# Raw expert weights in two places, loaded two experts ahead, and their load tables made one tile per partition

## The chip, the cores and the metric

The kernel runs on one core of one Trainium2 chip. The metric is the device time of one execution in microseconds; smaller is better. Engines are named as in the profile: PE (matmuls), DVE (vector), ACT (scalar), POOL (GpSimd), SP (which issues most of the DMAs here).

## What is computed

Two gated layers over x of 16 x 128 tokens with 512 features. The first three parts (cross attention with 16 heads, a ternary linear layer, a sigmoid attention over features) are not touched. The fourth is a mixture of 16 experts on 2048 tokens, with two shared experts:

```python
scores = jax.nn.sigmoid(xf @ gate_w.T)                 # [2048, 16]
...                                                    # best 2 of 4 groups, best 4 experts of these
cw = jnp.zeros((T, E), x.dtype).at[jnp.arange(T)[:, None], idx].add(w)
h = jax.nn.silu(jnp.einsum('td,edh->teh', xf, w1)) * jnp.einsum('td,edh->teh', xf, w3)
y = jnp.einsum('teh,ehd,te->td', h, w2, cw)
z = jax.nn.silu(xf @ sw1) * (xf @ sw3) @ sw2
return (y + z).reshape(b, s, d)
```

An expert has W1 and W3 of 512 x 352 and W2 of 352 x 512, all float32. The kernel computes y for the chosen four experts of a token only.

## The kernel before

**Order of the program.** Three blocks run one after the other: `attention_heads_and_ternary`, `attention_features`, `experts`. The last has two stages, `routing_and_shared_expert` and `expert_tiles`. Inside a stage every engine has its own list of instructions, written out by hand; semaphores are the only order between engines, and an engine that waits holds up all that stands behind on its list.

**Tiles.** Tokens are sorted by expert into tiles of 128 rows, each expert's share filled up to whole tiles; with these inputs 68 tiles are in use, in 17 trips of four (`UT`). Twelve experts get tiles. With tiles numbered from 0, an expert's first tile is one of 0, 1, 2, 7, 23, 28, 31, 35, 36, 44, 53, 62, so that three experts have one tile only (tiles 0, 1 and 35).

**A tile n in `expert_tiles`.** All products are made in three passes from a high and a low part of each operand. PE multiplies the rows by W1 and W3 (24 matmuls, `t_H`, L1738), transposes the rows of tile n+1 (`t_TX`, L1717), multiplies tile n-1 by W2 (`t_Y`, L62 to L64) and transposes the hidden rows of tile n (`t_TH`, L1750). ACT makes SiLU (L1783) and the high part of each operand, DVE the product (L1837) and the low parts; x of the next tile is L1760 on ACT and L1812 on DVE.

**The expert weights.** SP loads raw W1 and W3 into `r13` (L990) and raw W2 into `r2` (L995, L996); both are called `m_r` in the profile, and there is one place for each. ACT and DVE split them into `W13` and `W2` (`m_W`): W13 of tile n+1's expert during tile n (L1764 on ACT, L1816 on DVE), W2 of tile n's expert at the end of tile n (L1797, L1798; L1850, L1853). When tile n is the first of its expert, SP waits until W13 of that expert is split (`w13_lo`), so that `r13` is free, and issues W1 and W3 of the next expert; then it waits for the W2 split and issues W2. So a load starts at the first tile of the expert before.

**What a tile needs to know.** `m_meta` in SBUF holds for each tile whether it is the first of its expert, and the next expert; each engine reads these numbers into registers (a TENSOR_LOAD and a few register operations) and branches on them. DVE and ACT read one number at each tile (L1834, L1780), and two more at the start of a trip (L1829 and L1831 on DVE). They stand ahead of the tile's first instruction, the copy `t_wcol` (L1835) on DVE and the SiLU on ACT.

**Where `m_meta` is made.** In `routing_and_shared_expert` the shared expert runs as 24 chunks q: `hidden(q)` on PE, `gated(q)` on ACT and DVE, and after three of them `outer(u)` on PE. `hidden(q)` waits for `gated(q-2)`'s first step, because the banks A and B are double. DVE does the routing between chunks, by the table `between`; q = 10, 11 and 12 make the numbers of all 83 columns in every partition, as operations of 128 x 1328 elements. From q = 12 on DVE also makes rows for a one-hot product on PE (`table`, L1493 and L1495; PE's `tables`, L1268), which yields the row numbers of every tile.

Of the kernel before, what the change touches and what calls it, by code (L numbers as in the profile page):

```python
# [15 lines left out]
P = 128  # L16
# [20 lines left out]
IC = [P, P, I - 2 * P]  # L37

# [923 lines left out]
def experts(nc, c, gate_w, ebias, w1, w2, w3, sw1, sw2, sw3, out):  # L962
# [7 lines left out]
    with ExitStack() as st:  # L970
        def sb(name, shape, dt=F32):
            return st.enter_context(nc.sbuf_tensor(name, shape, dt))
        m = dict(meta=sb("m_meta", [1, 3, NT + 3], I32),
# [13 lines left out]
def load_expert(sp, m, w1, w3, e, done):  # L987

    for j, w in enumerate((w1, w3)):
        sp.dma_start(m["r13"][:, :, j, :], w[bass.ds(e, 1)].rearrange("e (k p) i -> p (e k) i", p=P)).then_inc(done, 16)  # L990


def load_expert_out(sp, m, w2, e, done):

    sp.dma_start(m["r2"][:, 0:2, :], w2[bass.ds(e, 1), 0:2 * P, :].rearrange("e (k p) i -> p (e k) i", p=P)).then_inc(done, 16)  # L995
    sp.dma_start(m["r2"][0:IC[2], 2, :], w2[bass.ds(e, 1), 2 * P:I, :].rearrange("e p i -> p (e i)")).then_inc(done, 16)  # L996

# [11 lines left out]
def routing_and_shared_expert(nc, c, m, gate_w, ebias, w1, w2, w3, sw1, sw2, sw3):  # L1009
# [4 lines left out]
    with ExitStack() as st:  # L1014
# [8 lines left out]
        XT = sb("XT", [P, 2, KC, NB * S], F32R)  # L1023
        r1, r3, r2 = m["r13"][:, :, 0, :], m["r13"][:, :, 1, :], m["r2"][:, :, :]
# [14 lines left out]
        J = NT + 3  # L1039
        iE = sb("r_iE", [P, E])  # L1040
        iJ = sb("r_iJ", [P, NT + 3])
# [21 lines left out]
        for W_, n, k, w in ((W1, "W1", KC, I), (W3, "W3", KC, I), (W2, "W2", 3, D)):  # L1063
# [11 lines left out]
        ti = early[:, NB * 20:NB * 20 + NT + 3].bitcast(I32)  # L1075
# [3 lines left out]
        first, nxt = big[:, NB * TOPK * E:NB * TOPK * E + J], big[:, NB * TOPK * E + J:]  # L1079
# [4 lines left out]
                                    "meta_ok", "pads_in"))  # L1084
        row_out = [sem(f"e_row_out{b}") for b in range(NX)]
# [22 lines left out]
        with nc.Block() as block:  # L1108
            @block.sync
            def _(sp):  # L1110
# [23 lines left out]
                sp.wait_ge(x2_in, 32)  # L1134
                for g in range(NG):
# [54 lines left out]
            def _(pe):  # L1190
# [6 lines left out]
                def logit(g):  # L1197
# [7 lines left out]
                    for k in range(KC):  # L1205
                        i = mm3(pe, L[0:E, :], lambda h_: gwT[:, h_, k, :],
                                lambda h_: XT[:, h_, k, g * GT:(g + 1) * GT], k == 0, k == KC - 1)
# [9 lines left out]
                def hidden(q):  # L1217
# [8 lines left out]
                    for W_, bk in ((W1[b], A[q % 2]), (W3[b], B[q % 2])):  # L1226
                        for k in range(KC):
                            x_ = mm3(pe, bk[0:IC[ch], :], lambda j: W_[:, j, k, cols],
                                     lambda j: XT[:, j, k, gr * GT:(gr + 1) * GT], k == 0, k == KC - 1)
# [42 lines left out]

                def counts():
# [31 lines left out]
            def _(act):  # L1305
# [20 lines left out]
                for t in range(NB):  # L1326
                    act.wait_ge(t_fill, t + 1)
                    act.activation(XT[:, 0, :, t * P:(t + 1) * P], T[t % 2][:, :].rearrange("p (k n) -> p k n", k=KC),
# [10 lines left out]
                for q in range(3, 3 * NU):  # L1339
# [8 lines left out]
                    if q == SPLIT_AT[2]:  # L1348
                        act.wait_ge(meta_ok, 1)
                    if q in SPLIT_AT:  # L1350
                        split_hi(1, SPLIT_AT.index(q))
                    if q in EXPERT_AT:
# [3 lines left out]
                        act.activation(m["W13"][:, 0, k, :, :], m["r13"][:, k, :, :], ACT.Copy).then_inc(x13_hi, 1)  # L1356

            @block.vector
            def _(dve):
                done = 1  # L1360

                def step(instr):
                    nonlocal done
                    done += 1
                    instr.then_inc(routed, 1)
# [9 lines left out]
                je = [P, J, E]  # L1375
                cmp = eq[:, :].rearrange("p (j e) -> p j e", j=J)
                ej = big[:, 0:J]
# [128 lines left out]
                def tile_experts():  # L1506

                    step(dve.tensor_tensor(cmp, upto.unsqueeze(1).to_broadcast(je), iJ[:, :].unsqueeze(2).to_broadcast(je),
                                           ALU.is_le))
                    step(dve.tensor_reduce(ej, cmp, AX.X, ALU.add))  # L1510
                    step(dve.tensor_scalar(ej, ej, float(E - 1), None, ALU.min))
                    step(dve.memset(first[:, 0:1], 1.0))
                    step(dve.tensor_tensor(first[:, 1:J], ej[:, 1:J], ej[:, 0:J - 1], ALU.not_equal))

                def next_candidates():

                    step(dve.tensor_scalar(far, nt, 0.5, 1000.0, ALU.is_lt, ALU.mult))
                    step(dve.tensor_tensor(far, far, iE[:, :], ALU.add))
                    step(dve.tensor_tensor(cmp, iE[:, :].unsqueeze(1).to_broadcast(je), ej.unsqueeze(2).to_broadcast(je),
                                           ALU.is_le))  # L1520
                    step(dve.tensor_scalar(cmp, cmp, 1000.0, None, ALU.mult))

                def next_expert():
                    step(dve.tensor_tensor(cmp, cmp, far.unsqueeze(1).to_broadcast(je), ALU.add))
                    step(dve.tensor_reduce(nxt, cmp, AX.X, ALU.min))
# [362 lines left out]
```

## Time and profile before

| | |
|---|---|
| median of 3 runs | 1371.61 us (1370.1 to 1372.55) |
| the profiled execution | 1371.29 us, of it 1369.6 us from first to last instruction |
| mean granted PE clock | 0.954 of 2.4 GHz |
| PE busy | 1230.6 us (90%) |
| DVE, ACT, POOL busy | 719.2, 553.2, 424.0 us |
| stage of routing and shared expert | about 584 to 844 us of the span |
| tiles of the experts | 846 to 1347 us |

PE is the engine that is busy nearly throughout, so what counts is where it stands still and where its clock is at the lower level. The profile gives for each instruction the idle time of its engine before it and who ended it.

### The profile page before, as it was taken

The page shows a single profiled execution, that of the slowest core. Times are in us where ns is not written, and L with a number is a line of the kernel's source. Part 1 is how long each engine was busy: PE and PEld are TensorE (multiplying, and loading weights), DVE is VectorE, ACT ScalarE, POOL GpSimd, SP SyncE. Part 2 cuts the span into 40 slices and gives each one's busy share as a digit, 9 for nine tenths or more (in the row PEclk, how much of TensorE's full clock was granted, in tenths as well). Part 3 has the DMA queues.
Part 4 walks back from the last instruction along what each step waited for, and adds up shares of the span by engine and source line. Part 5 has one row for each costly group of instructions (what it writes and reads, how often), then busy time and mean ns, then how long its engine had stood idle before and what let it go on. Part 6 is the DMA issues. An engine that isn't in the chain of part 4 may idle for free. (4 is left out here: it accounts for less than half of the span.)

```text
span 1369.6 us, 25480 instructions
## 1 busy us (share of the span) xinstructions
PE 1230.6 (90%) x7821; PEld 1034.4 (76%) x7822; DVE 719.2 (53%) x1443; ACT 553.2 (40%) x1430; POOL 424.0 (31%) x504
## 2 busy tenths in 40 slices
PE   6998999999997399969998998699999989999992
PEld 6876777777776177746776876699999878999992
DVE  5666655656645589953677643442334443424340
ACT  4543444444444188833121111543344443434341
POOL 1101211211211556540005721235444433444442
PEclk9999999999998699979999999899999999999997
DMA  9000000000000111143000204555446755545456
GB/s 326 25 16 19 17 1 18 17 1 17 1 2 1 33 45 38 38 141 118 0 1 0 94 31 137 159 129 100 77 80 141 195 142 116 132 86 135 86 140 169
DMA packets 53880, 103.62 MB, mean 76 GB/s; under 512 B 5126, under 2 KB 20998, under 8 KB 53750
## 3 DMA queue, kind: packets, MB, share of 16 engines
q1 hardware_dynamic: 38182, 65.78, 14.7%
q0 software_dynamic: 15632, 36.97, 14.3%
q8 instruction: 40, 0.66, 0.2%
q14 instruction: 26, 0.21, 0.1%
HBM read 75.99 MB, written 30.93 MB: 78 GB/s over the span
## 5 line engine op out<-in xcount | busy, mean ns | idle before, releaser
L1738 PE MATMUL t_H<-m_W,t_xT 128*128 128x352 f32 x1632 | 286.4, 332 | 16.7 <-DVE m_W L1816 13.9
L1738 PEld LDWEIGHTS t_H<-m_W,t_xT 128*128 128x128 f32 x1632 | 268.0, 193 | 18.7 <-DVE m_W L1816 14.8
L1705 POOL DMA_INDIRECT acc_d<-t_ys,t_sid x68 | 109.2, 1606 | 279.0 <-ACT t_ys L1767 191.5
L1783 ACT ACTIVATE t_sl<-t_H 128x352 f32<-128x352 f32 x68 | 31.5, 463 | 175.4 <-PE t_H L1738 173.7
L597 ACT ACTIVATE pr<-pr 128x128 f32<-128x128 f32 x256 | 76.0, 298 | 55.2 <-DVE pr L758 53.9
L62 PE MATMUL t_Y<-m_W,t_hT 128*128 128x512 f32 (+1 forms) x207 | 88.2, 426 | 9.4 <-DVE t_hT L1861 6.4
L1837 DVE TENSOR_TENSOR t_h<-t_H,t_sl 128x352 f32<-128x352 f32 x68 | 35.5, 523 | 106.5 <-ACT t_sl L1783 106.5
L1767 ACT ACTIVATE t_ys<-t_Y,t_wcol 128x512 f32<-128x512 f32 x69 | 47.3, 685 | 94.8 <-PE t_Y L64 94.8
L1859 DVE TENSOR_TENSOR t_hT<-t_TH,t_hT 128x256 fp32r<-128x256 f32 x68 | 28.7, 422 | 107.1 <-ACT t_hT L1804 105.9
L64 PE MATMUL t_Y<-m_W,t_hT 128*128 128x512 f32 (+1 forms) x207 | 82.3, 397 | 0.0
L63 PE MATMUL t_Y<-m_W,t_hT 128*128 128x512 f32 (+1 forms) x207 | 82.0, 396 | 0.0
L386 POOL TENSOR_TENSOR X<-X,upd 128x512 f32<-128x512 f32 x16 | 20.3, 1269 | 160.0 <-DVE upd L737 160.0
L373 POOL TENSOR_TENSOR tmp<-tmp,nhalf 128x2 f32<-128x2 f32 (+2 forms) x22 | 18.6, 846 | 143.0 <-DVE tmp L627 119.2
L1174 POOL TENSOR_SCALAR m_W<-m_W,bst 128x128 fp32r<-128x128 f32 x64 | 52.0, 830 | 34.5 <-PE eL L1268 34.4
L753 DVE TENSOR_REDUCE mx<-SC 128x4 f32<-128x512 f32 x64 | 43.7, 683 | 32.7 <-PE SC L517 32.6
L569 ACT ACTIVATE pT<-T 128x512 f32<-128x512 f32 x64 | 38.0, 594 | 53.9 <-PE T L423 53.6
L1323 ACT ACTIVATE ehT<-eh 128x512 fp32r<-128x512 f32 (+1 forms) x24 | 15.2, 632 | 93.9 <-DVE eh L1543 93.9
L62 PEld LDWEIGHTS t_Y<-m_W,t_hT 128*128 128x128 f32 (+1 forms) x207 | 39.2, 189 | 16.6 <-DVE m_W L1853 7.0
L1812 DVE TENSOR_TENSOR t_xT<-t_TX,t_xT 128x512 fp32r<-128x512 f32 x69 | 47.6, 690 | 4.8 <-ACT t_xT L1760 2.3
L597 ACT ACTIVATION_READ_ACCUMULATOR pr<-pr 128x1 f32 x256 | 47.8, 187 | 0.0
L845 DVE TENSOR_TENSOR as<-asg,as 128x512 fp32r<-128x512 f32 x66 | 44.2, 688 | 4.4 <-ACT as L901 4.4
L64 PEld LDWEIGHTS t_Y<-m_W,t_hT 128*128 128x128 f32 (+1 forms) x207 | 39.0, 188 | 9.7
(415 smaller groups left out, 3229.6 us busy)
## 6 DMA issues: line engine op xcount, KB each, us to landing
m_r<-in_L_ffn_w_dram SPq DMA_DIRECT2D x26, 704.0 KB, 5.1
m_r<-in_L_ffn_w_dram SPq DMA_DIRECT2D x13, 512.0 KB, 3.9
aCX<-in_ctx_dram SPq DMA_DIRECT2D x20, 256.0 KB, 2.6
rows_d<-before_w SPq DMA_DIRECT2D x17, 256.0 KB, 2.0
CT<-in_ctx_dram SPq DMA_DIRECT2D x8, 512.0 KB, 3.8
X<-in_x_dram SPq DMA_DIRECT2D x4, 1024.0 KB, 13.0
acc_d<-X SPq DMA_DIRECT2D x4, 1024.0 KB, 4.2
m_r<-in_L_ffn_sw_dram SPq DMA_DIRECT2D x4, 704.0 KB, 5.4
```

Of the source, the lines that this page charges most:

```text
L62: pe.matmul(out, lhs(0), rhs(0), start=first, stop=False)
L63: pe.matmul(out, lhs(0), rhs(1), start=False, stop=False)
L64: return pe.matmul(out, lhs(1), rhs(0), start=False, stop=last)
L569: act.activation(pT[:, t % 2, :, :].rearrange("p j m -> p (j m)"), src, ACT.Copy).then_inc(t_hi, 1)
L597: i = act.activation(pp, pp, ACT.Exp, scale=SCALE0, accum_out=sums[:, t // HQ % 2, at_:at_ + 1])
L753: dve.tensor_reduce(mx[:, t % 2, :], bk, AX.X, ALU.max).then_inc(s_out, 1)
L845: dve.tensor_tensor(s[:, m % KC, 1, :], sg[:, m % KC, :], s[:, m % KC, 0, :].bitcast(F32), ALU.subtract)\
L1174: i = pool.tensor_scalar(tab_a[t % SLOTS][:, k, :], iP.bitcast(F32), place_p[:, t, k:k + 1], None, ALU.is_equal)
L1705: pool.indirect_dma_start(out=m["acc_d"][:, :], out_offset=bass.IndirectOffsetOnAxis(ap=sid[:, b:b + 1], axis=0), in_=ys[:, b, :], in_offs ...
L1738: x_ = pe.matmul(bk[b % 2][:, 0:I], xT[:, b % 2, jx, k, :], W13[:, jw, k, j, :], start=k == 0 and jx == jw, stop=k == KC - 1 and jx == 1)
L1767: act.activation(ys[:, (b - 1) % UT, :], Y[(b - 1) % 2][:, :], ACT.Copy, scale=wcol[:, (b - 1) % UT:(b - 1) % UT + 1]).then_inc(y_evac, 1)
L1812: dve.tensor_tensor(xT[:, b % 2, 1, :, :], TX[:, :].rearrange("p (k t) -> p k t", k=KC), xT[:, b % 2, 0, :, :].bitcast(F32), ALU.subtract) ...
```

## The change

**Places.** `m_raw` holds two experts' raw W1, W3 and W2 side by side. The second place lies where the stage before keeps its transposed rows `XT`; so `XT` is laid out group by group, and the second expert is loaded when the two groups under it have been used for the last time. Before the tiles start, the experts of the first two groups of tiles are loaded; at the first tile of an expert SP issues the load of the expert after the next, into the place of the present one. SP now also waits for the load before to have landed.

**Numbers.** ACT, DVE and SP read which place: two more register loads at each tile on ACT and DVE, one more on SP. The addresses of the splits and loads come from a register.

**Tables.** In place of operations over 83 x 16 columns in every partition, each partition works out the numbers of one tile, in operations of 16 columns or 1, up to four at once without a wait (`tile_columns`, at q = 10). PE turns the four resulting columns into rows (`tile_rows`, after `hidden(11)`), and DVE writes them to `m_meta` (at q = 11). Nothing of this is left at q = 12.

```diff
-                 r13=sb("m_r13", [P, KC, 2, I]), r2=sb("m_r2", [P, 3, D]),
+        with ExitStack() as shortly:
+            m["raw"] = shortly.enter_context(nc.sbuf_tensor("m_raw", [P, 2, RAW], F32))
+        sb("m_raw_first", [P, RAW])
...
-        XT = sb("XT", [P, 2, KC, NB * S], F32R)
+        XT = sb("XT", [P, NG, 2, KC, GT], F32R)
...
@@ SP, routing stage @@
-                sp.wait_ge(meta_ok, 1)
-                e0 = sp.value_load(m["meta"][0:1, 2, 0:1], min_val=0, max_val=E - 1)
-                load_expert(sp, m, w1, w3, e0, x13_in)
-                load_expert_out(sp, m, w2, e0, x2_in)
-                sp.wait_ge(x2_in, 32)
+                sp.wait_ge(meta_ok, 2)
+                one, two = (sp.value_load(m["meta"][0:1, at:at + 1], min_val=0, max_val=E - 1) for at in (AT_ONE, AT_TWO))
+                load_expert(sp, m, w1, w3, one, slice(0, 1), x13_in)
+                load_expert_out(sp, m, w2, one, slice(0, 1), x2_in)
+                sp.wait_ge(ab_fill, 3 * (NG + 2))
+                sp.wait_ge(x13_in, 32)
+                load_expert(sp, m, w1, w3, two, slice(1, 2), x13_in)
+                sp.wait_ge(x2_in, 32)
+                load_expert_out(sp, m, w2, two, slice(1, 2), x2_in)
...
@@ PE, routing stage @@
+                def tile_rows():
+                    pe.wait_ge(meta_ok, 1)
+                    for n in range(4):
+                        i = pe.matmul(CP[0:1, n * P:(n + 1) * P], cols[:, n:n + 1], c["identF"][:, :], start=True, stop=True)
+                    i.then_inc(meta_ps, 1)
...
                             hidden(q)
                             if q == 7:
                                 counts()
+                            if q == 11:
+                                tile_rows()
...
@@ DVE, routing stage @@
+                def tile_columns():
+                    step(dve.tensor_scalar(filled, nt, 0.5, None, ALU.is_gt),
+                         dve.tensor_tensor(begin, upto, nt, ALU.subtract),
+                         dve.tensor_scalar(passed, upto, mine, None, ALU.is_le),
+                         dve.tensor_scalar(use, mine, float(UT), upto[:, E - 1:E], ALU.mult, ALU.is_lt))
...
-                           8: expert_starts, 9: table_rows, 10: tile_experts, 11: next_candidates, 12: next_expert}
+                           8: expert_starts, 9: table_rows, 10: tile_columns, 11: tile_rows}
...
@@ SP, tiles @@
+                            place = bass.ds(sp.value_load(m["meta"][0:1, bass.ds(n + AT_PLACE, 1)], min_val=0, max_val=1), 1)
                             with sp.If(first):
+                                sp.wait_ge(r13_in, 32 * (n + 2))
+                                sp.sem_inc(own_sp, 1)
                                 sp.wait_ge(w13_lo, 4 * (n + 1))
                                 sp.sem_inc(own_sp, 1)
-                                load_expert(sp, m, w1, w3, nxt, r13_in)
+                                load_expert(sp, m, w1, w3, nxt, place, r13_in)
+                                sp.wait_ge(r2_in, 32 * (n + 2))
+                                sp.sem_inc(own_sp, 1)
                                 sp.wait_ge(w2_lo, 2 * (n + 1) + 2)
                                 sp.sem_inc(own_sp, 1)
-                                load_expert_out(sp, m, w2, nxt, r2_in)
+                                load_expert_out(sp, m, w2, nxt, place, r2_in)
...
@@ DVE, tiles (ACT alike) @@
-                            this, first = first, dve.value_load(m["meta"][0:1, 0, bass.ds(n + 1, 1)], min_val=0, max_val=1)
+                            this, first = first, dve.value_load(m["meta"][0:1, bass.ds(n + 1, 1)], min_val=0, max_val=1)
+                            here, there = (bass.ds(dve.value_load(m["meta"][0:1, bass.ds(n + AT_PLACE + a, 1)], min_val=0, max_val=1), 1)
+                                           for a in range(2))
                             dve.tensor_copy(wcol[:, b:b + 1], wgt[:, bass.ds(n, 1)])
...
-                    dve.tensor_tensor(W13[:, 1, k, :, :], r13[:, k, :, :], W13[:, 0, k, :, :].bitcast(F32), ALU.subtract)\
+                    dve.tensor_tensor(W13[:, 1, k, :, :], raw13(m, place)[:, k, :, :], W13[:, 0, k, :, :].bitcast(F32), ALU.subtract)\
```

Of the changed kernel's PE list, this is the end of `hidden(11)` (banks `eB`) and the start of `hidden(12)` (`eA` with the second shared expert's weights `eW`); line numbers are those of the changed kernel, and `before_w` holds the four columns.

```order
L66 MATMUL eB<-XT,m_W 96x512
L67 MATMUL eB<-XT,m_W 96x512
L68 MATMUL eB<-XT,m_W 96x512
L1299 MATMUL eC<-identF,before_w 1x128 [waits e_meta_ok]
L1299 MATMUL eC<-identF,before_w 1x128 x3
L66 MATMUL eA<-XT,eW 128x512 [waits eb_out,ew_lo]
L67 MATMUL eA<-XT,eW 128x512
```

Before, `hidden(12)` stands directly behind `hidden(11)`; now four small matmuls that wait for DVE's `tile_columns` stand between.

On DVE the same place is q = 10 to q = 11. Before, between the steps of `gated(10)` (L1545) and `gated(11)` (L1543):

```order
L1545 TENSOR_TENSOR ehT<-eh,ehT 128x512 [waits eh_hi]
L1508 TENSOR_TENSOR before_w<-r_n,r_iJ 128x1328
L1510 TENSOR_REDUCE before_w<-before_w 128x83 [waits e_routed]
L1511 TENSOR_SCALAR before_w<-before_w 128x83 [waits e_routed]
L1512 MEMSET before_w 128x1 [waits e_routed]
L1513 TENSOR_TENSOR before_w<-before_w 128x82 [waits e_routed]
L1543 TENSOR_TENSOR eh<-eB,m_first 96x512 [waits eh_lo,ea_out,e_routed]
```

In the changed kernel 20 operations stand there, in eight groups; these are the first groups and the last three groups:

```order
L1542 TENSOR_SCALAR before_w<-r_n 128x16
L1543 TENSOR_TENSOR before_w<-r_n 128x16
L1544 TENSOR_SCALAR before_w<-r_n,r_tok 128x16
L1545 TENSOR_SCALAR before_w<-r_tok,r_n 128x1
L1546 TENSOR_SCALAR r_n<-before_w 128x16 [waits e_routed]
...
L1558 TENSOR_SCALAR before_w<-r_iE,before_w 128x16 [waits e_routed]
L1559 SCALAR_TENSOR_TENSOR before_w<-before_w 128x1
L1560 TENSOR_TENSOR before_w<-before_w,r_n 128x16 [waits e_routed]
L1561 TENSOR_REDUCE before_w<-before_w 128x1 [waits e_routed]
L1583 TENSOR_TENSOR eh<-eB,m_first 96x512 [waits eh_lo,ea_out]
```

Five operations, two of them wide, have become twenty narrow ones, and the last of them is what PE waits for.

On DVE in the tiles, between the low parts of tile n's hidden rows (L1909 and L1911) and the product of tile n+1 (L1887), the changed kernel has:

```order
L1911 TENSOR_TENSOR t_hT<-t_TH,t_hT 96x128
L1882 ISA
L1882 TENSOR_LOAD m_meta
L1882 ISA x2
L1883 TENSOR_LOAD m_meta
L1883 ISA x3
L1883 TENSOR_LOAD m_meta
L1883 ISA x2
L1885 REGISTER_ALU
L1885 COPY t_wcol<-m_wgt 128x1
L1887 TENSOR_TENSOR t_h<-t_H,t_sl 128x352 [waits t_silu]
```

Before, only the first of the three register loads (TENSOR_LOAD) stood there.

## Rows read from the trace of the kernel before

**Rows 1.** PE by time, tiles 9 and 13: start us, us, engine, line, operation.

```profile
927.36 4.10 PE L1738 MATMUL t_H<-m_W,t_xT 128*128 128x352 f32 x24
...
954.31 4.08 PE L1738 MATMUL t_H<-m_W,t_xT 128*128 128x352 f32 x24
```

**Rows 2.** The same view, tile 1 to tile 4; in brackets the idle before.

```profile
859.23 4.14 PE L1738 MATMUL t_H<-m_W,t_xT 128*128 128x352 f32 x24
...
864.45 0.48 PE L62 MATMUL t_Y<-m_W,t_hT 128*128 128x512 f32 x1 [0.64 <-DVE t_hT L1861]
...
874.88 6.11 PE L1738 MATMUL t_H<-m_W,t_xT 128*128 128x352 f32 x24 [7.76 <-DVE m_W L1816]
...
890.64 0.47 PE L62 MATMUL t_Y<-m_W,t_hT 128*128 128x512 f32 x1 [2.47 <-DVE t_hT L1861]
...
893.07 4.10 PE L1738 MATMUL t_H<-m_W,t_xT 128*128 128x352 f32 x24
```

**Rows 3.** The same view, tile 35 to tile 38.

```profile
1104.70 4.14 PE L1738 MATMUL t_H<-m_W,t_xT 128*128 128x352 f32 x24
...
1117.82 5.84 PE L1738 MATMUL t_H<-m_W,t_xT 128*128 128x352 f32 x24 [6.10 <-DVE m_W L1816]
...
1134.16 0.47 PE L62 MATMUL t_Y<-m_W,t_hT 128*128 128x512 f32 x1 [3.31 <-DVE t_hT L1861]
...
1137.67 4.57 PE L1738 MATMUL t_H<-m_W,t_xT 128*128 128x352 f32 x24
```

**Rows 4.** SP by time: two of the issues of raw W1 and W3.

```profile
866.68 0.93 SPq L990 DMA_DIRECT2D m_r<-in_L_ffn_w_dram  x2
...
1107.30 0.95 SPq L990 DMA_DIRECT2D m_r<-in_L_ffn_w_dram  x2
```

**Rows 5.** DVE by time, round the trip ends after tiles 7 and 11.

```profile
925.49 0.15 DVE L1835 COPY t_wcol<-m_wgt 128x1 f32 x1 [1.37 <-issue]
...
925.99 0.68 DVE L1812 TENSOR_TENSOR t_xT<-t_TX,t_xT 128x512 fp32r<-128x512 f32 x1
...
951.71 0.15 DVE L1835 COPY t_wcol<-m_wgt 128x1 f32 x1 [2.21 <-issue]
...
958.92 0.53 DVE L1837 TENSOR_TENSOR t_h<-t_H,t_sl 128x352 f32<-128x352 f32 x1 [2.31 <-ACT t_sl L1783]
```

**Rows 6.** Register loads on DVE, 948 to 955 us: duration ns, first and last start.

```profile
L1829 DVEq TENSOR_LOAD <-m_meta x1: 305/305/305, 949.4 to 949.4; - x1
...
L1834 DVEq TENSOR_LOAD <-m_meta x1: 374/374/374, 950.9 to 950.9; - x1
```

**Rows 7.** PE by time, in the stage of routing and shared expert.

```profile
717.86 0.40 PE L64 MATMUL eB<-XT,m_W 128*96 128x512 f32 x1
...
725.34 0.47 PE L62 MATMUL eY<-m_W,ehT 128*128 128x512 f32 x1 [1.42 <-issue]
...
742.72 1.15 PE L1268 MATMUL eL<-m_W 128*128 128x240 f32 x4 [3.30 <-DVE m_W L1495]
744.32 1.18 PE L1268 MATMUL eL<-m_W 128*128 128x240 f32 x4 [0.45 <-DVE m_W L1495]
```

**Rows 8.** DVE by time, where it makes the tables for the loads.

```profile
719.29 1.63 DVE L1508 TENSOR_TENSOR before_w<-r_n,r_iJ 128x1328 f32<-128x1328 f32 x1
...
723.17 0.69 DVE L1543 TENSOR_TENSOR eh<-eB,m_first 96x512 f32<-96x512 f32 x1
...
736.57 1.53 DVE L1524 TENSOR_TENSOR before_w<-before_w,r_n 128x1328 f32<-128x1328 f32 x1
```

**Rows 9.** DVE by time: three small operations without a wait between, then the next.

```profile
583.74 0.19 DVE L109 TENSOR_TENSOR mean<-bst 128x16 f32<-128x16 f32 x1 [0.30 <-PEq L812]
...
584.15 0.17 DVE L112 TENSOR_SCALAR mean<-mean 128x16 f32<-128x16 f32 x1
```

**Rows 10.** By stretch: its us, busy us of PE, PEld, DVE, ACT, POOL; clock, DMA, GB/s.

```profile
742.80:749.70 6.90, 6.46 (x19) 4.71 (x20) 6.10 (x9) 1.58 (x2) 5.73 (x6) 0.51 0.01 2
...
1135.00:1139.00 4.00, 4.00 (x15) 3.35 (x14) 0.20 (x1) 1.23 (x3) 0.06 (x1) 0.57 0.50 172
```

More of the change, by code:

```diff
@@ L37 @@
 IC = [P, P, I - 2 * P]
+RAW = 2 * KC * I + 3 * D
+AT_FIRST, AT_NEXT, AT_PLACE, AT_USE = 0, NT + 1, 2 * NT + 1, 3 * NT + 2
+AT_ONE, AT_TWO, AT_TRIPS = AT_USE + TRIPS, AT_USE + TRIPS + 1, AT_USE + TRIPS + 2
+META = AT_TRIPS + 1
 class Count:
@@ L1355, in _ @@
                         act.wait_ge(tab_used, NB)
-                        act.activation(m["W13"][:, 0, k, :, :], m["r13"][:, k, :, :], ACT.Copy).then_inc(x13_hi, 1)
+                        act.activation(m["W13"][:, 0, k, :, :], r13[:, k, :, :], ACT.Copy).then_inc(x13_hi, 1)
             @block.vector
@@ L1360, in _, with step @@
                 done = 1
-                def step(instr):
+                def step(*instrs):
                     nonlocal done
-                    done += 1
-                    instr.then_inc(routed, 1)
+                    for instr in instrs:
+                        instr.then_inc(routed, 1)
+                    done += len(instrs)
                     dve.wait_ge(routed, done)
@@ L1374, in _ @@
                 pl = run[:, 1, :, :]
-                je = [P, J, E]
-                cmp = eq[:, :].rearrange("p (j e) -> p j e", j=J)
-                ej = big[:, 0:J]
+                filled, begin, passed, both, cand, col = (spare_cols[:, n * E:(n + 1) * E] for n in range(6))
+                here, nxt, half = (col[:, n:n + 1] for n in (4, 5, 6))
                 def best_groups():
@@ new lines, in tile_rows @@
+                def tile_rows():
+                    dve.wait_ge(meta_ps, 1)
+                    for n, (at, w) in enumerate(((AT_FIRST, NT + 1), (AT_NEXT, NT), (AT_PLACE, NT + 1), (AT_USE, TRIPS))):
+                        dve.tensor_scalar(m["meta"][:, at:at + w], CP[0:1, n * P:n * P + w], float(E - 1), None, ALU.min)
+                    dve.tensor_scalar(m["meta"][:, AT_ONE:AT_ONE + 1], here[0:1, :], float(E - 1), None, ALU.min)
+                    dve.tensor_scalar(m["meta"][:, AT_TWO:AT_TWO + 1], nxt[0:1, :], float(E - 1), None, ALU.min)
+                    step(dve.tensor_scalar(half[0:1, :], upto[0:1, E - 1:E], 1.0 / UT, 0.5 - 0.5 / UT, ALU.mult, ALU.add))
+                    dve.tensor_scalar(m["meta"][:, AT_TRIPS:AT_TRIPS + 1], half[0:1, :], ROUND, -ROUND, ALU.add, ALU.add)\
+                        .then_inc(meta_ok, 1)
@@ L1616, in bank @@
             return [st.enter_context(nc.psum_tensor(f"{name}{i}", [P, 512], F32)) for i in range(n)]
-        rowid, wgt, r13, r2, W13, W2 = (m[n] for n in ("rowid", "wgt", "r13", "r2", "W13", "W2"))
+        rowid, wgt, W13, W2 = (m[n] for n in ("rowid", "wgt", "W13", "W2"))
+        sb("t_raw_second", [P, RAW])
         sid = sb("t_sid", [P, UT], U32)
@@ L1760, in x_hi, with w13 @@
                     act.activation(xT[:, b % 2, 0, :, :], TX[:, :].rearrange("p (k t) -> p k t", k=KC), ACT.Copy).then_inc(tx_hi, 1)
-                def w13():
+                def w13(place):
                     for k in range(KC):
-                        act.activation(W13[:, 0, k, :, :], r13[:, k, :, :], ACT.Copy).then_inc(w13_hi, 1)
+                        act.activation(W13[:, 0, k, :, :], raw13(m, place)[:, k, :, :], ACT.Copy).then_inc(w13_hi, 1)
                 def y_out(b):
@@ L1787, in _ @@
                                 act.wait_ge(r13_in, 32 * (n + 2))
-                                w13()
+                                w13(there)
                             with act.Else():
@@ L1842, in _ @@
                                     dve.wait_ge(w13_hi, 4 * (n + 1) + k + 1)
-                                    w13_k(k)
+                                    w13_k(k, there)
                             with dve.Else():
```

139 lines of the change are left out of this document (73 added, 66 removed).

## The prediction

> **What bounds the kernel.** I read the page first: PE is busy 90% of the span, so I looked for the places where PE stands still or runs at the lower clock. Then I read PE in order of time through the tiles. In the steady state four tiles take 954.31 - 927.36 = 26.95 us, 6.74 each, without a gap [rows 1]. Twice it is otherwise. From the start of tile 1 to that of tile 4 it takes 893.07 - 859.23 = 33.84 us instead of 20.2 [rows 2]: PE waits 7.76 us for split W13 ahead of tile 2, 2.47 us for a hidden row that stands behind the W2 split on ACT and DVE, and the 24 matmuls of tile 2 take 6.11 us instead of 4.14, as the clock has fallen. From tile 35 to tile 38 it takes 1137.67 - 1104.70 = 32.97 us [rows 3], with waits of 6.10 and 3.31 us and again one slow group. Both follow an expert of one tile. The issues on SP say why: the weights that tile 2 lacks were asked for at 866.68, when tile 1 was already running, and those of tile 36 at 1107.30, inside tile 35 [rows 4]. Elsewhere an expert has at least two tiles, and its successor's load is back in time.
>
> The third place is in the routing stage. PE stops for 3.30 and 0.45 us ahead of the one-hot products [rows 7], since DVE makes the load tables first (from 736.57, [rows 8]); behind it the clock is at half for 6.9 us [rows 10].
>
> **The change, part by part.**
>
> *Late loads.* With two places the load that started at 866.68 starts one expert earlier, and so do the others; tiles 2 and 36 find their weights split as soon as ACT and DVE come to them. What is late next is the splitting itself: tiles 0, 1 and 35 each split W2 for themselves and W13 for the next one. Tile 0 does this today with everything landed, and PE waits 0.64 us for it [rows 2]. I keep that, and give tile 1, which starts with DVE behind, 0.9. Front: 33.84 - 20.2 - 0.64 - 0.9 = 12.1 us, rounded to 12.0. Tile 35 gets 0.9 too, and it is also the last of a trip, where the register loads (below) come on top of the split: 1.6. Middle: 32.97 - 20.2 - 0.9 - 1.6 = 10.3 us. The start of tile 0 stays as it is. Bounds: no wait left gives 13.6 + 12.8 = 26.4, and 2 us more in each place gives 18.
>
> *Register loads.* DVE now reads three numbers ahead of a tile instead of one, and five instead of three at a trip's start. Three loads start 950.9 - 949.4 = 1.5 us apart from first to last, so one costs 0.75 us [rows 6], and two more 1.5. In a tile inside a trip DVE idles 2.31 us for SiLU behind them [rows 5], so they are hidden, and what they cost without that cover is 1.5 us a tile. At a trip's start they already take all the time: the copy stands 2.21 us behind the last work for "issue", at 951.71. From the copy to the end of the next x on DVE it takes 925.99 + 0.68 - 925.49 = 1.18 us [rows 5]. With 1.5 us more this x would be ready at 954.39, and PE wants it at 954.31 [rows 1]: 0.1 us a trip. Where a split stands in the tile before the trip's start, DVE comes later. After tile 7 x was ready at 926.67 and PE began at 927.36; with 1.5 more it begins at 928.17, 0.8 us late. Such trip ends are those after tiles 7, 23 and 31 (W2) and 27 and 43 (W13); the one after 35 is in the middle's sum. So 5 x 0.8 + 10 x 0.1 = 5.0 us lost. Bounds: nothing (if the loads run ahead) and twice that.
>
> The Trainium skill, page "DMA: Bandwidth & Descriptors", section "Latency and other measured facts", gives a floor of some 600 ns for a tensor_load. Here the load itself is shorter (305 to 374 ns [rows 6]), and with its register operations it takes 0.75 us; by the page's figure two cost 1.2, the loss would be about 3 us, and the estimate of the time about 1351.
>
> *Tables.* At q = 12 the work from 736.57 goes away, and the rows for PE are made at once. PE's wait of 3.30 + 0.45 us and the half clock behind it go: of 6.9 us PE is busy 6.46 [rows 10], which at the full clock is 3.2 us less. Gain 6.95 us. But `tile_rows` puts a wait on PE in front of `hidden(12)`. PE comes to it at 718.26 [rows 7]; DVE only starts `tile_columns` at 719.29, where the old table code starts today [rows 8]. Three operations of 128 x 16 issued together take 584.15 - 583.74 = 0.41 us [rows 9], about 0.21 for a group and 0.1 for each further one; 20 in eight groups take 8 x 0.21 + 12 x 0.1 = 2.9 us. So PE stands still until 722.2, 4 us, makes four small products (0.45 us; four of 240 columns took 1.15 at the low clock [rows 7], and these have 128) and begins `hidden(12)` 4.5 us later than today. Queued behind it is `outer(3)`, which today waits 1.42 us for DVE before 725.34 [rows 7]; that wait is swallowed, so it starts 3.1 us late. A stand of 4 us is longer than the 3.30 and 3.31 us after which the clock fell [rows 3, 7, 10], so I expect it to fall here too. The price is half the time at the low clock: 1.7 us after tile 37 (4.0 us at 0.57) and 3.2 at 742.8; I take 2.1, nearer to the first, since here no second wait follows. Together 5.2 lost, 6.95 won: 1.75 us gained. Bounds: if the clock holds 3.85; if each of the 20 operations takes 0.21 us and the clock costs 3.2, a loss of 0.7.
>
> *Free.* The second load before the tiles lies under the shared expert's last chunks on PE, and SP's stores behind it are wanted only when all is stored. The layout of `XT` keeps the same 512 columns in a row for PE. SP's extra register load and waits stand where SP has been idle.
>
> *Sum.* 12.0 + 10.3 - 5.0 + 1.7 = 19.0 us. The profiled execution took 1371.29, which gives 1352.3; it lies 0.3 below the median, so 1352.6.
>
> **The rivals.**
>
> *All cover holds.* The register loads run ahead on DVE and ACT while they wait, and the clock holds through the stand at 718: 26.4 less some 2 of splitting, plus 3.85, gives 28 us, 1343.5. For it speaks that inside a trip they are covered; against it the 2.21 us of "issue" at the trip's start.
>
> *The loads stay late.* SP takes its list in order, and a load of W1 and W3 now stands behind waits for the load before and for the W2 split. If tile 36's weights still came after tile 35 began, only the tables and the register loads would change: 1370 to 1375. Against it: the W2 split that SP waits for ends in the same tile, and two experts ahead of tile 36 are four tiles, some 27 us.
>
> *The register loads decide, and it is slower.* They stand ahead of the first instruction of every tile, on ACT and DVE. Inside a trip the cover is the 2.31 us of idle on DVE, and some 0.9 more: x is ready about 958.92 + 1.2 = 960.1, and PE wants it at 954.31 + 6.74 = 961.05 [rows 1, 5]. So two loads may cost 3.2 us, 1.6 each. Above that each tenth costs 0.2 us a tile; with some 60 tiles the 24 us of the other terms are eaten up at 1.8 us a load, and at 2.0 the time is near 1395. The place is the copy at L1835. For it: at a trip's start the copy waits 2.21 us for nothing else. Against it: 0.75 us a load in the steady state.
>
> *Gathers get in the way.* The loads of three experts now run close together at the start, beside the gathers of rows on the same DMA engines; a gather that lands two tiles late would cost PE up to 3 us there, 1356. I count this within the main case.
>
> **How the numbers follow.** Main case 0.72, from 1347 to 1361 (the sum with the register loads from 0 to 10, the tables from -0.7 to 3.9, the gathers). All cover holds 0.15, from 1342 to 1347. Loads stay late 0.07. Register loads on the path of every tile 0.06. The range of 1344 to 1361 takes the main case and part of the second: about 0.8. From no change 0.2% can be told here, 2.7 us: faster below 1368.9, slower above 1374.4. Faster: 0.72 + 0.15 and 0.01 of the late loads, 0.88; same 0.05, from the late loads; slower 0.06 + 0.01.
>
> **What would show it.** In the profile after: no wait for `m_W` longer than 1.5 us ahead of `t_H` between tiles 0 and 4 and 35 and 38; both stretches at 21.7 to 23 us; raw weights never named as releaser of ACT. At trip starts the copy on DVE some 3.7 us behind the last work instead of 2.21, and a gap on PE ahead of `t_H` after tiles 7, 23, 27, 31 and 43. In the routing stage a PE wait of about 4 us at the four products into `eC`, a lower clock behind it, and none ahead of the one-hot products. I am wrong if PE still waits for a load, if the gaps stand at every tile, or if the wait at `eC` is 6 us or more.

## The result, and the profile after

The changed kernel takes 1357.9 us (1356.34 to 1361.29), the kernel before, timed beside it, 1372.08 (1370.1 to 1373.06): a ratio of 0.9904, 95% interval 0.9889 to 0.9919, or 14.2 us less. Timed a second time in another set it came to 1360.91 against 1371.61, ratio 0.9922 (0.9895 to 0.9948). The profiled execution took 1358.05 us with a span of 1356.2, which is 13.4 less than before.

PE by time, in the kernel after. The line numbers are those of the new file: `t_H` is L1784, `t_TX` L1763, the four table products L1299.

```profile
718.17 0.40 PE L68 MATMUL eB<-XT,m_W 128*96 128x512 f32 x1
722.67 1.87 PE L1299 MATMUL eC<-identF,before_w 128*1 128x128 f32 x8 [4.11 <-DVE before_w L1561]
724.47 0.80 PE L66 MATMUL eA<-XT,eW 128*128 128x512 f32 x1
...
844.52 0.63 PE L1763 MATMUL t_TX<-identF,m_first 128*128 128x128 f32 x4 [1.62 <-PEq L1125]
...
856.72 4.12 PE L1784 MATMUL t_H<-m_W,t_xT 128*128 128x352 f32 x24
...
861.96 0.47 PE L66 MATMUL t_Y<-m_W,t_hT 128*128 128x512 f32 x1 [0.68 <-DVE t_hT L1911]
...
864.71 4.12 PE L1784 MATMUL t_H<-m_W,t_xT 128*128 128x352 f32 x24
...
869.58 0.47 PE L66 MATMUL t_Y<-m_W,t_hT 128*128 128x512 f32 x1 [0.32 <-DVE t_hT L1911]
...
879.11 4.14 PE L1784 MATMUL t_H<-m_W,t_xT 128*128 128x352 f32 x24
...
884.35 0.66 PE L1763 MATMUL t_TX<-identF,m_first 128*128 128x128 f32 x4 [1.09 <-DMA m_first<-rows_d,m_pos]
...
943.07 4.10 PE L1784 MATMUL t_H<-m_W,t_xT 128*128 128x352 f32 x24
...
970.48 4.11 PE L1784 MATMUL t_H<-m_W,t_xT 128*128 128x352 f32 x24
...
1096.96 4.12 PE L1784 MATMUL t_H<-m_W,t_xT 128*128 128x352 f32 x24
...
1109.15 0.47 PE L66 MATMUL t_Y<-m_W,t_hT 128*128 128x512 f32 x1 [0.49 <-DVE t_hT L1911]
...
1112.47 0.55 PE L1796 MATMUL t_TH<-identF,t_h 128*128 128x128 f32 x3 [0.98 <-DVE t_h L1887]
...
1119.89 4.09 PE L1784 MATMUL t_H<-m_W,t_xT 128*128 128x352 f32 x24
...
1225.03 4.12 PE L1784 MATMUL t_H<-m_W,t_xT 128*128 128x352 f32 x24 [0.85 <-DVE m_W L1864]
```

Read it in four steps. From tile 1 to tile 4 it is 879.11 - 856.72 = 22.39 us where [rows 2] had 33.84: the wait of 7.76 for split W13 is gone, the clock stays, and two short waits for hidden rows remain. From tile 35 to 38 it is 22.93 against 32.97 [rows 3]. In the routing stage PE stands for 4.11 us ahead of the products into `eC`, and nothing is left of the waits of 3.30 and 0.45 [rows 7]. And where nothing is split, a trip from tile 13 to 17 takes 970.48 - 943.07 = 27.41 us instead of 26.95 [rows 1].

SP's issues of raw W1 and W3 after. Each is now for the expert after the next: the weights of tile 2's expert are asked for at 850.41, inside tile 0, where before they were at 866.68 [rows 4]; the issue at 865.51 is already for the expert of tile 7.

```profile
850.41 1.00 SPq L1004 DMA_DIRECT2D m_raw<-in_L_ffn_w_dram  x2
...
865.51 0.98 SPq L1004 DMA_DIRECT2D m_raw<-in_L_ffn_w_dram  x2
```

DVE by time after: the first and the last operation that makes the columns, then the start of the trip at tile 12.

```profile
719.59 0.26 DVE L1542 TENSOR_SCALAR before_w<-r_n 128x16 f32<-128x16 f32 x1
...
722.45 0.17 DVE L1561 TENSOR_REDUCE before_w<-before_w 128x1 f32<-128x16 f32 x1
...
937.54 0.28 DVE L1911 TENSOR_TENSOR t_hT<-t_TH,t_hT 96x128 fp32r<-96x128 f32 x1
941.76 0.15 DVE L1885 COPY t_wcol<-m_wgt 128x1 f32 x1 [3.94 <-issue]
...
942.26 0.68 DVE L1860 TENSOR_TENSOR t_xT<-t_TX,t_xT 128x512 fp32r<-128x512 f32 x1
```

The columns take 722.62 - 719.59 = 3.03 us. The copy stands 3.94 us behind the last work (2.21 in [rows 5]), and x of tile 13 is ready at 942.94, 0.13 before PE takes it. The stretch behind PE's stand, by stretch as in [rows 10], shows the clock, first in the kernel before, then after:

```profile
722.30:725.80 3.50, 2.08 (x10) 1.42 (x9) 2.57 (x9) 1.11 (x2) 3.50 (x7) 1.00 0.00 0
...
722.30:725.80 3.50, 3.13 (x11) 1.98 (x12) 2.48 (x12) 0.63 (x1) 3.50 (x7) 0.51 0.00 0
```

The loads of a place on DVE (duration in ns, first and last start), once at the start of the trip, once inside it:

```profile
L1883 DVEq TENSOR_LOAD <-m_meta x1: 741/741/741, 939.9 to 939.9; - x1
...
L1883 DVEq TENSOR_LOAD <-m_meta x2: 300/302/303, 944.8 to 945.5; - x2
```

Inside the trip two loads start 0.7 us apart, as in [rows 6]; at its start one of them takes 0.74. At the start of the trip at tile 64 none is slow; this is PE, the loads and DVE there:

```profile
1301.39 4.13 PE L1784 MATMUL t_H<-m_W,t_xT 128*128 128x352 f32 x24
...
L1883 DVEq TENSOR_LOAD <-m_meta x2: 300/301/302, 1305.4 to 1306.1; - x2
...
1306.84 0.15 DVE L1885 COPY t_wcol<-m_wgt 128x1 f32 x1 [3.50 <-issue]
...
1307.34 0.68 DVE L1860 TENSOR_TENSOR t_xT<-t_TX,t_xT 128x512 fp32r<-128x512 f32 x1
```

The last view is what PE waited for ahead of `t_TX` (us in total, times, longest), as far as it was the landing of a gather: 2.5 us in the tiles, before 1.6.

```profile
PE t_TX L1763 <- DMA m_first<-rows_d,m_pos: 2.0, 4, 1.1
...
PE t_TX L1763 <- DMA t_later<-rows_d,m_pos: 0.5, 1, 0.5
```

### The profile page after: what moved, and what is told of

It reads as the page before. It is cut to its first block and busy times, and to the rows that moved or that the text cites. A ratio compares the mean times of both kernels' runs of the same rounds, so it can differ in the third digit from the quotient of the medians.

```text
span 1356.2 us, 26974 instructions
## 1 busy us (share of the span) xinstructions
PE 1230.3 (91%) x7829; PEld 1027.0 (76%) x7830; DVE 710.0 (52%) x1454; ACT 552.5 (41%) x1430; POOL 420.1 (31%) x504
## 5 line engine op out<-in xcount | busy, mean ns | idle before, releaser
L1784 PE MATMUL t_H<-m_W,t_xT 128*128 128x352 f32 x1632 | 281.5, 328 | 5.5 <-issue 3.0
L1784 PEld LDWEIGHTS t_H<-m_W,t_xT 128*128 128x128 f32 x1632 | 262.6, 189 | 12.1 <-issue 4.3
L1885 DVE COPY t_wcol<-m_wgt 128x1 f32 x68 | 10.5, 154 | 134.3 <-issue 134.3
L1909 DVE TENSOR_TENSOR t_hT<-t_TH,t_hT 128x256 fp32r<-128x256 f32 x68 | 28.7, 423 | 93.2 <-ACT t_hT L1852 92.0
L1197 POOL TENSOR_SCALAR m_W<-m_W,bst 128x128 fp32r<-128x128 f32 x64 | 49.1, 786 | 35.8 <-PE eL L1291 35.7
L1887 DVE TENSOR_TENSOR t_h<-t_H,t_sl 128x352 f32<-128x352 f32 x68 | 35.4, 521 | 45.9 <-ACT t_sl L1831 45.9
L1641 DVE SCALAR_TENSOR_TENSOR X<-eY,tg,X 128x512 f32<-128x512 f32 x32 | 23.8, 751 | 49.1 <-PE eY L68 49.0
L66 PEld LDWEIGHTS t_Y<-m_W,t_hT 128*128 128x128 f32 (+1 forms) x207 | 39.0, 188 | 11.7 <-issue 3.8
```

Of the source, the lines that this page charges most:

```text
L66: pe.matmul(out, lhs(0), rhs(0), start=first, stop=False)
L1197: i = pool.tensor_scalar(tab_a[t % SLOTS][:, k, :], iP.bitcast(F32), place_p[:, t, k:k + 1], None, ALU.is_equal)
L1784: x_ = pe.matmul(bk[b % 2][:, 0:I], xT[:, b % 2, jx, k, :], W13[:, jw, k, j, :], start=k == 0 and jx == jw, stop=k == KC - 1 and jx == 1)
L1887: dve.tensor_tensor(h[:, :], H3[b % 2][:, 0:I], sl[:, :], ALU.mult).then_inc(hmul, 1)
```

## The experiments

Times vary by some us from run to run, partly ahead of everything that the change touches: PE starts the routing stage at 582 to 587 us of the span. So beside the times the table gives stretches of the profiled executions, from the start of a tile's `t_H` to that of another (us). "Rest" is tiles 4 to 35 plus 38 to 67.

| kernel | median, ratio to before (95%) | 1 to 4 | 35 to 38 | rest |
|---|---|---|---|---|
| before | 1372.08 | 33.84 | 32.97 | 408.96 |
| changed | 1357.9, 0.9904 (0.9889 to 0.9919) | 22.39 | 22.93 | 419.60 |
| loads one expert ahead | 1382.17, 1.0063 (1.0043 to 1.0083) | 35.95 | 31.15 | 418.08 |
| before, two more register loads | 1378.75, 1.0050 (1.0031 to 1.0069) | 34.53 | 31.49 | 416.14 |
| place loaded in the branch | 1355.1, 0.9871 (0.9848 to 0.9895) | 22.27 | 22.21 | 416.98 |
| products one chunk later | 1349.41, 0.9839 (0.9814 to 0.9863) | 22.31 | 23.06 | 418.60 |
| gather early | 1355.28, 0.9878 (0.9848 to 0.9908) | 22.27 | 23.20 | 416.52 |
| place packed | 1353.69, 0.9857 (0.9826 to 0.9888) | 21.75 | 21.52 | 413.87 |
| gather and scatter swapped | 1390.8, 1.0131 (1.0104 to 1.0159) | 22.16 | 22.74 | 441.52 |
| packed, products later | 1344.44, 0.9816 (0.9784 to 0.9847) | 21.52 | 21.52 | 415.99 |
| packed, products later, gather early | 1336.25, 0.9752 (0.9718 to 0.9787) | 21.77 | 21.51 | 407.73 |

**The early loads undone.**

```diff
-dve.tensor_reduce(after, cand, AX.X, ALU.min).then_inc(meta_ok, 1)
+dve.tensor_copy(after, nxt).then_inc(meta_ok, 1)
...
-load_expert(sp, m, w1, w3, two, slice(1, 2), x13_in)
...
-place = bass.ds(sp.value_load(...), 1)
+place = bass.ds(sp.value_load(...) * -1 + 1, 1)
```

(and the counts that SP waits for, one load lower)

> The changed kernel with both places, the new tables and all register loads, but each expert's raw weights asked for one expert ahead, as in the kernel before. If the early loads are what made tiles 1 to 4 and 35 to 38 shorter, the waits for split W13 ahead of tiles 2 and 36 come back with some 7.8 and 6.1 us, both stretches are back near 34 and 33 us, and the time is some 21.5 us above the changed kernel: about 1379, slower than the kernel before. If having two places is enough in itself (a load need not wait for the split of the one before), the stretches stay at 22 to 23 us and the time at about 1358.

PE by time at tiles 1, 2, 4 and 36 of this kernel:

```profile
859.07 5.67 PE L1779 MATMUL t_H<-m_W,t_xT 128*128 128x352 f32 x24 [2.09 <-DVE m_W L1859]
...
876.34 5.61 PE L1779 MATMUL t_H<-m_W,t_xT 128*128 128x352 f32 x24 [8.71 <-DVE m_W L1859]
...
895.02 4.85 PE L1779 MATMUL t_H<-m_W,t_xT 128*128 128x352 f32 x24
...
1125.86 5.46 PE L1779 MATMUL t_H<-m_W,t_xT 128*128 128x352 f32 x24 [6.50 <-DVE m_W L1859]
```

Both waits are back, a third of 2.09 us stands ahead of tile 1, and the kernel is slower than before. Two places alone win nothing; what wins is that the load starts an expert earlier. The row also prices the rest of the change: without the early loads it loses.

**Register loads alone, on the kernel before.**

```diff
 this, first = first, dve.value_load(...)
+for a in range(2):
+    dve.value_load(m["meta"][0:1, 0, bass.ds(n + a, 1)], min_val=0, max_val=1)
```

(the same on ACT)

> The kernel before with two more register loads ahead of each tile on ACT and on DVE, whose values nothing uses. If the register loads are the whole loss at the trips' ends, this costs 0.45 us at a trip without a split and 0.5 to 1.3 at one with a split, together 6 to 10 us: 1378 to 1382. If the loss comes from the two places or from their transfers, it costs at most 2 us. If the loads stand on the path of every tile it costs 30 us or more.

PE by time, tiles 13 and 17:

```profile
957.76 4.11 PE L1738 MATMUL t_H<-m_W,t_xT 128*128 128x352 f32 x24
...
985.06 4.14 PE L1738 MATMUL t_H<-m_W,t_xT 128*128 128x352 f32 x24
```

A trip without a split takes 27.30 us, 0.35 more than [rows 1]; outside the two stretches the loads cost 416.14 - 408.96 = 7.2 us. That is most of the 10.6 us which the changed kernel loses there, with no second place and no earlier transfer in sight.

**The loads put where they are used.**

```diff
-here, there = (bass.ds(dve.value_load(...n + AT_PLACE + a...), 1) for a in range(2))
 ...
 with dve.If(first):
+    there = bass.ds(dve.value_load(...n + AT_PLACE + 1...), 1)
 ...
 with dve.If(this):
+    here = bass.ds(dve.value_load(...n + AT_PLACE...), 1)
```

(the same on ACT)

> The changed kernel with the two loads of a place's number on ACT and DVE moved from the head of every tile into the branches that use them, so that a tile that splits nothing makes none. If the loads at a trip's start are what costs 0.46 us at each trip without a split and about 0.5 to 1.3 at the others, the normal trip is back to 26.95 us and the time falls by 6 to 9 us, to 1349 to 1352; the loads inside the branches stand behind work of 0.6 to 0.7 us that is already running and cost at most 0.1 a split. If the trips are longer because ACT and DVE read from a place that a register names, or because loads of two experts share the DMA engines with the gathers, nothing changes: 1358. If a load inside a branch delays the split by its full 0.7 us on ACT and on DVE, about half is given back at some 30 splits: 1356 or more.

The trip from tile 13 to 17 is back to 26.93 us, but a tile that splits W13 for the next one took 7.33 to 7.37 us (tiles 6, 22, 43, 61) instead of 6.93 to 6.98: of the expected 6 to 9 us only 2.6 are left in the rest. The loads in the branch delay the split, so the third case held beside the first.

**The place packed into the first-tile number.**

```diff
+dve.scalar_tensor_tensor(out=new, in0=place, scalar=1.0, in1=new, op0=ALU.add, op1=ALU.mult)
 ...
-here, there = (...)
 with dve.If(first):
+    there = bass.ds(first // 2, 1)
```

(and so for `here`, on ACT and on SP)

> The changed kernel with the place packed into the number that says whether a tile is its expert's first (0, 1 or 2), so that ACT and DVE make as many register loads as in the kernel before and divide in registers, inside the branches. If the loads are the loss at the trips' ends, the normal trip is back to 26.95 us as with the loads in the branches, and the 0.4 us that each split lost there is not paid: the time falls by 6 to 9 us, to 1349 to 1352. If reading the raw weights through a place named in a register costs the time, or the division costs as much as a load, it stays at 1355 as with the loads in the branches, or at 1358.

The rest falls by 419.60 - 413.87 = 5.7 us, and the split tiles cost 7.01 to 7.05. That is the register loads' part with nothing put in their place. It did not go all the way back to 408.96. The split tiles are still 0.2 us above those of the kernel before (6.81 to 6.86), and PE's waits for gathered rows ahead of `t_TX` grew from 2.5 to 3.9 us:

```profile
PE t_TX L1764 <- DMA t_later<-rows_d,m_pos: 2.0, 2, 1.8
PE t_TX L1764 <- DMA m_first<-rows_d,m_pos: 1.9, 5, 0.7
```

PE, less delayed by its x, now meets the gathers earlier.

**The products into `eC` one chunk later.**

```diff
-if q == 11:
+if q == 12:
     tile_rows()
```

(in PE's list only)

> The changed kernel with the four small products of the tables behind the next hidden chunk on PE instead of ahead of it. If the stand of 4.11 us and the half clock behind it were the price that the tables paid, PE starts that chunk at 718.3 instead of 724.5, the products come at about 723.9 with their columns ready since 722.6, and the time falls by 5 to 6 us, to about 1352.5. If DVE, not PE, sets the end of this stage (its hidden rows follow the columns), PE only waits further on, ahead of the output products: a gain of 1 to 3 us, 1355 to 1357.

PE by time: the products, `outer(3)` right behind them, and the first transpose of the tiles.

```profile
720.14 1.03 PE L1299 MATMUL eC<-identF,before_w 128*1 128x128 f32 x8
...
721.10 0.50 PE L66 MATMUL eY<-m_W,ehT 128*128 128x512 f32 x1
...
835.03 0.63 PE L1763 MATMUL t_TX<-identF,m_first 128*128 128x128 f32 x4 [1.62 <-PEq L1125]
```

There is no wait. From `outer(3)` to `t_TX` it takes 113.93 us, in the changed kernel 844.52 - 730.74 = 113.78; so the whole gain lies ahead of it. From the start of the chunk before (708.8 here, 712.9 there) to `t_TX` it is 126.2 against 131.6 us: 5.4 us, as the theory of PE's stand said. The median is 8.5 us lower; the profiled execution was 4 us ahead already at the start of that chunk, which is the spread named above.

**The gather ahead of the scatter's waits.**

```diff
 pool.wait_ge(zeroed, n * 2 + UT)
+gather(pool, m, b)
 ...
 pool.indirect_dma_start(out=m["acc_d"][:, :], ...)     # scatter
-gather(pool, m, b)
```

> The changed kernel with the gather of the rows of a tile issued on GpSimd as soon as their place is free, ahead of the scatter of the finished tile instead of behind it. In the changed kernel the last register load at six trip starts takes 0.74 us on DVE and 0.94 on ACT instead of 0.30, and ends 0.42 us behind the end of a gather's issue that runs beside it. If the gather's issue holds the load up, moving it away brings these loads back to 0.30 us, the normal trip from 27.41 to about 27.0 us, and with the waits of PE for gathered rows (some 7.6 us in all, not all on the path) the time falls by 4 to 8 us: 1350 to 1354. If the loads are slow because five engines read the same table at a trip's start, they stay at 0.74 and 0.94 and only the gather waits can go: 1354 to 1357. If the issue of the gather now stands in front of the scatter and the scatters become late, up to 3 us slower.

The waits for gathered rows ahead of `t_TX` are gone, and the rest falls by 3.1 us. (The 7.6 us of the expectation count each such wait on PE and once more on PE's weight loads; PE itself waited 2.5.) The routing stage, which this edit does not touch, took longer here: the lower clock behind PE's stand lasted on, in the view by stretch:

```profile
723.70:730.20 6.50, 6.50 (x20) 4.55 (x21) 2.13 (x10) 0.63 (x1) 4.69 (x8) 0.52 0.00 0
```

But the slow register loads stayed. POOL by time and the load, in the changed kernel:

```profile
937.32 1.61 POOL L1751 DMA_INDIRECT acc_d<-t_ys,t_sid  x1 [3.53 <-ACT t_ys L1813]
939.23 1.00 POOL L1015 DMA_INDIRECT t_later<-rows_d,m_pos  x1 [0.31 <-issue]
```

and with the early gather:

```profile
939.00 1.60 POOL L1752 DMA_INDIRECT acc_d<-t_ys,t_sid  x1 [3.00 <-ACT t_ys L1813]
...
941.71 1.00 POOL L1015 DMA_INDIRECT t_later<-rows_d,m_pos  x1 [0.79 <-POOL m_pos L1744]
```

```profile
L1883 DVEq TENSOR_LOAD <-m_meta x1: 725/725/725, 941.6 to 941.6; - x1
```

The gather's issue went from before the slow load to after its start, the load stayed slow. What did not move against it is the scatter: its issue ends at 938.93 and 940.60, the slow load starts 1.0 us later in both. My theory that the gather's issue holds the loads up fell. The other case, five engines that read one table at a trip's start, fits the time as well; the next run is for the scatter.

**Gather and scatter swapped.**

```diff
 pool.wait_ge(y_evac, n + 4)
+gather(pool, m, b)
 pool.indirect_dma_start(out=m["acc_d"][:, :], ...)     # scatter
-gather(pool, m, b)
```

> The changed kernel with the gather and the scatter of GpSimd swapped behind the same wait, so that the scatter is issued 1.0 us later. With the gather issued early, the slow register loads at the trip starts did not go: in both kernels they start within 0.5 us of the first packet of a scatter, which moves from about 939.5 to 940.5 here, while the slow loads start at 939.7 to 939.9. If the start of the scatter's transfers holds the loads up, these loads take 0.30 us, the normal trip falls from 27.41 to about 27.0 us and the time by 3 to 4 us against the changed kernel in the same call or the trace. If the loads are slow for their place in the program (the third of a tile's head at a trip's start, beside PE's transposes), they stay at 0.74 and 0.94 us and the normal trip at 27.4.

POOL by time at the start of the trip at tile 12, and register loads on DVE there:

```profile
944.44 1.00 POOL L1015 DMA_INDIRECT m_first<-rows_d,m_pos  x1 [3.41 <-DMA acc_d<-t_ys,t_sid]
945.75 1.60 POOL L1752 DMA_INDIRECT acc_d<-t_ys,t_sid  x1 [0.30 <-issue]
```

```profile
L1877 DVEq TENSOR_LOAD <-m_meta x1: 780/780/780, 948.3 to 948.3; - x1
...
L1883 DVEq TENSOR_LOAD <-m_meta x2: 300/301/302, 951.0 to 951.7; - x2
```

The loads that had been slow take 0.30 us, and another is slow, 0.9 us behind the new end of the scatter's issue. So the cause moved with the scatter, as the first theory said. The gain did not come: another load of the same trip's start is slow instead, and loads at the heads of ordinary tiles are hit too, which also speaks against five engines at a trip's start.

The kernel lost 33 us for a reason that I had not seen. By its list POOL waits for the landing of a scatter before the next pair (3.41 us here; in the changed kernel it waited for ACT instead). With that wait POOL needs 6.64 us from one gather to the next (937.80 to 944.44), nearly the 6.7 us that a tile takes PE, so that hardly any slack is left. At tiles 8, 45 and 63, where raw weights are being loaded, the wait is 6.97 to 7.21 us:

```profile
916.61 1.00 POOL L1015 DMA_INDIRECT m_first<-rows_d,m_pos  x1 [7.10 <-DMA acc_d<-t_ys,t_sid]
```

PE then waits 5.28 us for this gather and 16.4 us in all for rows; these three tiles lose 19 of the 22 us that the rest lost, and 6 us more stand behind the last tile. In this profile 5 us of the 33 stand ahead of the tiles, which the swap does not touch.

**All that helped, together.** Packed number and later products; then the early gather too.

> Two of the three edits of the fastest kernel so far: the place packed into the first-tile number and the four products behind the next hidden chunk, with the gather left behind the scatter. If the early gather is worth the waits for rows on PE, this is 3 to 5 us slower than with all three, 1339 to 1342. If the packed number leaves little for the gather, 1336 to 1338.

> Three edits on the changed kernel together: the place packed into the first-tile number, the four products of the tables behind the next hidden chunk, and the gather issued ahead of the scatter. If each takes away a loss of its own, the gains add up: 6 to 9, 6 to 8 and 2 to 5 us, so 1336 to 1344. If the packed number already takes the loads away from the gather, the gather's part is only that of the waits for rows: 1341 to 1346. If one of the three returns the others' gains, it is no faster than the products alone, 1349.

With three edits the kernel takes 1336.25 us, 35.4 less than before and 24.7 less than the changed kernel timed beside it.

The gains add up, and more: the gather is worth 3.1 us on the changed kernel and 415.99 - 407.73 = 8.3 on the packed one, whose PE comes earlier for its rows. The rest is now 1.2 us shorter than before the change, and the kernel before waited for gathers as well. I had put it at 1336 to 1344, and the run without the early gather at 1339 to 1342; that one came to 1344.44.

**The changed kernel again.**

> The changed kernel as it is, timed beside the others on the same chip: 1358, or 14 us below the kernel before, as the first time. If the chip of this call gives another distance, the edits are to be compared with this run and not with the first one.

It lay 10.7 us below the kernel before, in an interval that overlaps the first.

## Why the prediction was right, and where not

It said 1352.6, in a range of 1344 to 1361, and faster with 0.88; it is faster, at 1357.9. In spans the sum promised 19.0 us and 13.4 came.

- **Late loads, front and middle: right.** 12.0 and 10.3 forecast, 33.84 - 22.39 = 11.45 and 32.97 - 22.93 = 10.04 measured. PE waits for `m_W` in neither stretch, and ACT never for raw weights (15.0 us in three places before). The run with the loads one expert ahead shows that it is the earlier load and not the second place. What is late next is the splitting, as said: 0.68, 0.32, 0.49 and 0.98 us.
- **Tables: right, the size in part by luck.** The stand at `eC` was put at 4 us and is 4.11, the columns at 2.9 and are 3.03, the clock does fall (0.51 behind it, where it was 1.00 before), the waits ahead of the one-hot products are gone. The four products were put at 0.45 us and take 1.80 at the low clock (722.67 to 724.47; 0.96 at full clock in the run with later products); it did not show, since the lower clock cost `hidden(12)` behind them only some 0.5 us (724.47 to 730.74, against 718.13 to 723.92 before), where 2.1 had been allowed. From 718.26 [rows 7] to the first `t_TX` at 846.05 it took 127.8 us, now from 718.57 to 844.52 125.95: 1.8 us gained, 1.75 forecast. That depends on how long the clock stays down: with the same order on PE, the runs with the early gather and with the packed place needed 127.4 and 127.5 us for this stretch, a gain of only some 0.3, since there the lower clock lasted over 6 us. I had seen that `tile_rows` stands ahead of `hidden(12)` and priced it at 5.2 us; moving it gave 5.4.
- **Register loads: the step that was mis-sized.** The sum had 5.0 us. A trip end beside a split lost 0.46 to 0.86 us at the five places named (0.8 forecast; at tiles 28 and 44 counted with the tile behind). Wrong was "0.1 us a trip" for the others: at tiles 12, 16, 20, 48 and 60 a trip lost 0.45 to 0.50 (0.33 to 0.41 with the loads alone). Two things were left out. One of the later loads falls on the start of a scatter and takes 0.74 instead of 0.30, so that the copy stands 3.94 us behind the last work, where 3.7 was forecast. That accounts for the loss of such a trip: at tile 64, whose loads stand as far behind `t_H`, no load is slow, the copy stands 3.50 behind, x is ready 6.63 us after the start of `t_H` instead of 7.07 (935.87 to 942.94) at tile 12, and the trip lost 0.03. Tiles 40 and 56 lost no more than 0.04. And tile 52, the first of its trip, splits W13 itself, behind its delayed x: PE waits 0.85 us ahead of tile 53, and 1.1 are lost there. By the loads alone the term is 7.2 us, and 5.7 by taking them out of the changed kernel. The figure of the Trainium skill ("DMA: Bandwidth & Descriptors", "Latency and other measured facts", a floor of some 600 ns for a tensor_load) would have made the term smaller still. This case's traces do not bear it out: a load takes 0.30 us here, 0.7 with its register operations, and 0.72 to 0.94 by itself beside a scatter.
- **Gathers: counted at nothing, worth up to 3.1 us.** The rival named them with up to 3 us and I left them in the main case's range, not in its sum. The 3.1 us are what the early gather takes away from the changed kernel; a part was there before (PE waited 1.6 us, now 2.5). 1.09 us stand at tile 5's rows (884.35) alone. Raw weights are loaded beside them there, as the rival said: the DMA engines are busy for 0.87 of the time from 878.0 to 884.4, and 0.48 from 945 to 951. No run takes the loads away and leaves the gathers, so their share stays open.
- **Not forecast:** from the first `t_TX` to tile 1 it took 12.20 us instead of 13.18. In all runs with the early loads tile 0 takes 8.26 to 9.71 us, 9.86 before. Most of it is the clock, which falls during its 24 matmuls: they took 6.84 us at a mean of 0.56 before, 6.05 at 0.65 after and 5.42 at 0.73 in the run with later products. So I do not count it to the change.

The account: 11.45 + 10.04 + 1.8 + 1.0 for tile 0, less 10.6 in the rest and 0.3 ahead of the tables, gives 13.4, the difference of the spans. The 10.6 are 7.2 of register loads and some 3 of gathers within the error of such pieces; they do not simply add, since a PE that comes later waits less for rows.

Of the rivals, all cover holds fell by the register loads and by the clock behind the stand; loads that stay late and register loads on the path of every tile are each ruled out by the rows of tiles 1 to 4 and of 13 to 17, where three of four tiles still take 6.7 us.

## What to carry to other kernels

A prefetch pays by the moment at which it is issued; a second buffer that is filled no earlier wins nothing. Numbers that an engine reads into registers ahead of its first instruction are work on that engine at every loop start, where no idle time covers them: pack them into a number that is read anyway, or read them where a wait stands. When a new step puts a wait into a busy engine's list, look for the next place down the list where its input is ready already; here that one line was worth 5.4 us.

## What the hardware showed that I had not expected

A register load that starts about 1 us behind the end of a scatter's issue, as its transfers begin (issue to 938.93, first packets at about 939.5 in the changed kernel above), is slow in most cases. Counted over the register loads of DVE, ACT and SP after 860 us, by whether they start 0.4 to 1.2 us after the end of a scatter's issue on POOL:

```
                     inside: loads, over 0.4 us, mean    outside: loads, over 0.4 us, mean
before                  20      16     0.68 us             336       3     0.29 us
changed                 48      38     0.68                641       8     0.28
gather early            49      38     0.67                643      16     0.29
swapped                104     101     0.79                588      21     0.29
```

Counted in the same way behind the issues of gathers, 1 of 37 loads is over 0.4 us in the changed kernel and 4 of 58 in the swapped one. The loads of DVE and ACT that are held end at the same time, and the swap moved the slow loads with the scatter. What the load and the scatter share stays open.
